# Output projection and first norm interleaved with the first 96 codebook lookup slots of a transformer layer (one core)

## What is computed

```python
q, k, v = proj(wq), proj(wk), proj(wv)            # 32 heads of 32, rotary on q and k
out = softmax(causal(q @ k.T / sqrt(32))) @ v
x = layernorm(x + out @ wo.T)                      # the part that the change moves
Wg, Wu, Wd = codebook[idx_gate], codebook[idx_up], codebook[idx_down]
h = silu(x @ Wg.T) * (x @ Wu.T)                    # inner width 2752
x = layernorm(x + h @ Wd.T)
```

## Time and profile before

| | |
|---|---|
| median of 3 runs | 7037.45 us (7036.92 to 7038.21) |
| the profiled execution: its time / its span | 7038.14 us / 7036.0 us |
| TensorE matmul busy | 6852.8 us, 97% of the span |
| VectorE / ScalarE / GpSimd busy | 4982.9 (71%) / 3672.3 (52%) / 5063.2 (72%) |
| TensorE on the chain that ended last | 63% of the span |

### The profile page before, as it was taken

How to read it: one execution, slowest core, us unless ns; L and a number is a source line. 1 busy time by engine, 2 the same in 40 slices (tenths; PEclk the granted TensorE clock), 3 DMA queues, 4 the chain that set the end, 5 groups by cost and what they waited for, 6 DMA issues and landing times.

```text
span 7036.0 us, 109336 instructions
## 1 busy us (share of the span) xinstructions
PE 6852.8 (97%) x29072; PEld 4331.6 (62%) x29072; DVE 4982.9 (71%) x11788; ACT 3672.3 (52%) x6498; POOL 5063.2 (72%) x5316
## 2 busy tenths in 40 slices
PE   7999999999999999999999999999999999999998
PEld 3444666665466656666666666666666666666664
DVE  3320777775299877788877888778887788877864
ACT  0000777774177755555555555555555555555541
POOL 7777777777777777777777777777777777777760
PEclk9999999999999999999999999999999999999999
DMA  4232111112233323333332333333333233333321
GB/s 127 63 90 49 30 33 32 33 31 58 46 88 90 77 63 72 66 70 72 70 71 64 72 74 72 69 66 71 71 71 70 64 72 72 70 72 67 71 59 48
DMA packets 472442, 462.10 MB, mean 66 GB/s; under 512 B 231120, under 2 KB 347728, under 8 KB 467536
## 3 DMA queue, kind: packets, MB, share of 16 engines
q10 hardware_dynamic: 287072, 396.73, 20.0%
q0 software_dynamic: 169984, 22.10, 7.8%
q1 hardware_dynamic: 14832, 36.84, 1.4%
HBM read 398.07 MB, written 57.15 MB: 65 GB/s over the span
## 4 chain that ended last, share of the span: by engine, by line
PE 63%; DVE 2%; issue 1%; ACT 1%; DMA 0%; DVEq 0%; ACTq 0%
PE ps L414 33%; PE ps L442 17%; PE ps L460 9%; PE ps L425 4%; DVE onehot L964 1%; DVE picked L972 1%; PE ps L431 0%; ACT onehot L738 0%; ACT onehot L742 0%; PE ps L534 0%; DVE small L1015 0%; ACT arena L824 0%; DMA arena<-code_low 0%; DVEq L191 0%; DVE big L956 0%
## 5 line engine op out<-in xcount | busy, mean ns | idle before, releaser
L201 POOL DMA_INDIRECT raw<-in_codebook_dram,idx_sb x5312 | 5063.0, 953 | 1763.9 <-issue 1760.9
L414 PE MATMUL ps<-onehot,table 128*128 128x512 f32 x11776 | 3149.5, 416 | 55.4 <-DVE picked L972 28.7
L964 DVE TENSOR_SCALAR_CACHE_REDUCE onehot<-arena,small 128x512 fp32r<-128x512 f32 x3685 | 2514.1, 743 | 786.7 <-PE ps L414 759.2
L414 PEld LDWEIGHTS ps<-onehot,table 128*128 128x128 f32 x11776 | 2172.1, 188 | 944.3 <-issue 312.6
L738 ACT ACTIVATE onehot<-arena,small 128x512 fp32r<-128x512 f32 x2211 | 1435.4, 713 | 1078.7 <-PE ps L414 974.2
L742 ACT ACTIVATE onehot<-onehot,small 128x512 fp32r<-128x512 f32 x2211 | 1425.2, 708 | 0.0
L442 PE MATMUL ps<-big,arena 128*128 128x512 f32 (+1 forms) x2816 | 1281.2, 592 | 1.3 <-DVE big L956 1.3
L972 DVE SCALAR_TENSOR_TENSOR picked<-arena,small,ps 128x512 fp32r<-128x512 f16 x1472 | 1032.2, 743 | 52.7 <-PE ps L414 37.8
L442 PEld LDWEIGHTS ps<-big,arena 128*128 128x128 f32 (+1 forms) x2816 | 524.2, 187 | 514.0 <-issue 477.5
L877 DVE TENSOR_REDUCE small<-ps 128x1 f32<-128x384 f32 (+7 forms) x512 | 374.2, 752 | 434.7 <-PE ps L304 434.6
L460 PE MATMUL ps<-arena 128*128 128x512 f32 (+1 forms) x1408 | 646.0, 595 | 2.2 <-ACT arena L714 1.1
(11 more groups left out here) (70 smaller groups left out, 3117.4 us busy)
## 6 DMA issues: line engine op xcount, KB each, us to landing
arena<-code_low ACTq DMA_DIRECT2D x738, 256.0 KB
arena<-code_high ACTq DMA_DIRECT2D x738, 128.0 KB
raw<-in_codebook_dram,idx_sb POOLq DMA_INDIRECT x5312
gathered_units<-raw SPq DMA_DIRECT2D x40, 512.0 KB
arena<-gathered_units ACTq DMA_DIRECT2D x20, 1024.0 KB
queries_keys<-arena ACTq DMA_DIRECT2D x16, 1024.0 KB, 4.0
arena<-queries_keys ACTq DMA_DIRECT2D x32, 512.0 KB
big<-in_xT_dram ACTq DMA_DIRECT2D x4, 2048.0 KB, 17.4
```

What stands on the lines that cost most here:

```text
L201: pool.indirect_dma_start(raw[:, s, n, :], None, codebook, bass.IndirectOffsetOnAxis(ap=idx_sb[:, s, n:n + 1], axis=0),).then_inc(gathered ...
L414: last = mm(ps[:, bank + c, :], table[:, k, c, :], onehot[:, k, :], start=(k == 0), stop=(k == KLO - 1))
L964: dve.tensor_scalar(onehot[:, k, :], lo_sb[:, s % 2, :], kp_sb[:, k:k + 1], None, ALU.is_equal, ALU.add, accum_out=hits[:, k:k + 1]).then_ ...
```

## The change

The x1 stage no longer stands ahead of the 96 slots. Each of the 16 blocks of tokens gets six slots (BESIDE = 6, numbered q = 0 to 5). TensorE's 16 products of the block are cut by PARTS into 4, 4, 3, 3, 2 and 0, each cut placed ahead of that slot's look-up. The look-ups all use banks 4, 5 and wait for the pick of the slot before; banks 0, 1 take the projection and banks 2, 3 the transposes. VectorE's sum and statistics stand behind slot 4's work, its normalising behind slot 5's. The block's transposes stand behind the fold of slot q = 1 of the next block and ScalarE's copy at q = 2. ScalarE's square root is at q = 5. ScalarE issues the code loads first and the `sel` and `d_raw` loads behind them, all now right after attention.

```diff
+BESIDE = 3 * SLOTS // SB
+PARTS = (0, 4, 8, 11, 14, 16, 16)
...
-            def project(k):
-                past(pe, sum_ready, k - 1)
-                for h in range(2):
-                    for g in range(NG):
-                        last = mm(ps[:, 4 * (k % 2) + h, :], big1[:, g, k * P:(k + 1) * P], wo_sb[:, g, h * N:(h + 1) * N],
-                                  start=(g == 0), stop=(g == NG - 1))
-                last.then_inc(wo_done, 1)
+            def project(k, n0, n1):
+                if n0 == 0:
+                    past(pe, sum_ready, k)
+                for n in range(n0, n1):
+                    h, g = divmod(n, NG)
+                    last = mm(ps[:, h, :], big1[:, g, k * P:(k + 1) * P], wo_sb[:, g, h * N:(h + 1) * N],
+                              start=(g == 0), stop=(g == NG - 1))
+                if n1 == 2 * NG:
+                    last.then_inc(wo_done, 1)
...
-            for unit in range(3):
-                for s in range(SLOTS):
-                    look_up(unit * SLOTS, s, 4 - 4 * (s % 2), 1)
+            pe.wait_ge(wo_in, 16)
+            pe.wait_ge(o_copied, 2 * ROUNDS * PASSES)
+            for k in range(SB):
+                for q in range(BESIDE):
+                    if PARTS[q] < PARTS[q + 1]:
+                        project(k, PARTS[q], PARTS[q + 1])
+                    unit, s = divmod(k * BESIDE + q, SLOTS)
+                    look_up(unit * SLOTS, s)
+                    if k == 0 and q == 0:
+                        pe.wait_ge(sel_ready, 1)
                     if s:
                         fold(unit * SLOTS, unit, s - 1)
                     elif unit:
                         fold(unit * SLOTS - SLOTS, unit - 1, SLOTS - 1)
+                    if k and q == 1:
+                        turn_x1(k - 1)
+                if k == 0:
+                    pe.wait_ge(d_in, 16)
+                    for h in range(CS):
+                        last = nc.tensor.transpose(ps[0:HALF, 2 + h // 4, (h % 4) * P:(h % 4 + 1) * P],
+                                                   d_raw[:, h, :], id_sb[:, :])
+                    last.then_inc(turn_done, 1)
+            turn_x1(SB - 1)
+            pe.wait_ge(x1T_ready, SB)
```

ScalarE and VectorE:

```diff
+            act.wait_ge(o_copied, 2 * ROUNDS * PASSES)
             act.wait_ge(lo_out, 32)
             for s in range(2):
                 load_codes(0, s)
+            act.dma_start(sel_raw, sel).then_inc(sel_in, 16)
+            act.wait_ge(unit_ready, 1)
+            act.dma_start(d_raw, units[0, :, 0:CS * HALF].rearrange("p (h i) -> p h i", h=CS)).then_inc(d_in, 16)
             near(0, 0)
+            for k in range(SB):
+                for q in range(BESIDE):
+                    unit, s = divmod(k * BESIDE + q, SLOTS)
...
+                    if k == 1 and q == 0:
+                        turned(1, HALF, 2)
+                    if k and q == 2:
+                        copy_x1(k - 1)
+                    if q == BESIDE - 1:
+                        deviation(k)
                     near(unit * SLOTS, s + 1)
+            copy_x1(SB - 1)
...
+            for k in range(SB):
+                for q in range(BESIDE):
+                    unit, s = divmod(k * BESIDE + q, SLOTS)
+                    look_up(unit * SLOTS, s)
+                    if q == BESIDE - 2:
+                        norm_sums(k)
+                    if q == BESIDE - 1:
+                        norm(k)
```

More of the change, by code:

```diff
@@ L375, in _ @@
                 weigh(PASSES - 1, ROUNDS - 1, o, False)
-            def project(k):
-                past(pe, sum_ready, k - 1)
-                for h in range(2):
-                    for g in range(NG):
-                        last = mm(ps[:, 4 * (k % 2) + h, :], big1[:, g, k * P:(k + 1) * P], wo_sb[:, g, h * N:(h + 1) * N],
-                                  start=(g == 0), stop=(g == NG - 1))
-                last.then_inc(wo_done, 1)
+            def project(k, n0, n1):
[7 more added lines that the diff above has]
+                    last.then_inc(wo_done, 1)
             def turn_x1(k):
                 pe.wait_ge(x1_ready, k + 1)
-                past(pe, x1T_ready, k - 1)
+                past(pe, x1T_ready, k)
+                if k == 0:
+                    pe.wait_ge(d_ready, 1)
                 for e in range(KT):
-                    last = nc.tensor.transpose(ps[:, 4 * (k % 2) + 2 + e // 4, (e % 4) * P:(e % 4 + 1) * P],
+                    last = nc.tensor.transpose(ps[:, 2 + e // 4, (e % 4) * P:(e % 4 + 1) * P],
                                                x1_blk[:, k % 2, e * P:(e + 1) * P], id_sb[:, :])
                 last.then_inc(x1T_done, 1)
[L395 to L402, removed]
             def look_up(first, s, bank=4, held=0):
@@ L682, in load_block, with copy_x1 @@
                 act.dma_start(x_blk[:, k % 2, :], x_nat[k * P:(k + 1) * P, :]).then_inc(x_in[k % 2], 16)
[L684 to L693, removed]
+            def copy_x1(k):
+                act.wait_ge(x1T_done, k + 1)
+                act.copy(big1[:, :, k * P:(k + 1) * P],
+                         ps[:, 2:4, :].rearrange("p h (e s) -> p (h e) s", e=4)).then_inc(x1T_ready, 1)
+                if k + 2 < SB:
+                    load_block(k + 2)
             def load_gate_up(u, count):
@@ L779, in _ @@
                 load_codes(0, s)
-            turned(1, HALF, 2)
-            act.wait_ge(sel_ready, 1)
+            act.dma_start(sel_raw, sel).then_inc(sel_in, 16)
+            act.wait_ge(unit_ready, 1)
+            act.dma_start(d_raw, units[0, :, 0:CS * HALF].rearrange("p (h i) -> p h i", h=CS)).then_inc(d_in, 16)
             near(0, 0)
-            for unit in range(3):
-                for s in range(SLOTS):
+            for k in range(SB):
+                for q in range(BESIDE):
+                    unit, s = divmod(k * BESIDE + q, SLOTS)
                     next_codes(unit, unit * SLOTS, s)
@@ L924, in _, with norm_sums @@
                     copy_o(PASSES - 1, u, o)
-            for k in range(SB):
+            def norm_sums(k):
                 dve.wait_ge(wo_done, k + 1)
@@ L929, in _ @@
                 x_v = x_blk[:, k % 2, :].rearrange("p (h d) -> p h d", h=2)
-                dve.tensor_tensor(x_v, ps[:, 4 * (k % 2):4 * (k % 2) + 2, :], x_v, ALU.add).then_inc(sum_ready, 1)
+                dve.tensor_tensor(x_v, ps[:, 0:2, :], x_v, ALU.add).then_inc(sum_ready, 1)
                 dve.wait_ge(sum_ready, k + 1)
-                past(dve, x1T_done, k - 1)
                 for h in range(2):
@@ L937, in _, with norm @@
                 dve.bn_aggr(meanvar, stats.rearrange("p n k -> p (n k)")).then_inc(var_ready, 1)
+            def norm(k):
+                past(dve, x1T_done, k - 1)
                 dve.wait_ge(std_ready, k + 1)
@@ L997, in _ @@
                 one_hot(0, 0, k)
-            for unit in range(3):
-                for s in range(SLOTS):
-                    look_up(unit * SLOTS, s, 4 - 4 * (s % 2))
+            for k in range(SB):
[6 more added lines that the diff above has]
+                        norm(k)
             lookup_step(0, HALF, 3 * SLOTS)
```

## The result

The changed kernel takes 6995.1 us (median of 4 runs, 6993.79 to 6998.43) where the kernel before took 7037.5 (7036.92 to 7038.21) beside it: a ratio of 0.994, 95% interval 0.9923 to 0.9958, 42.4 us less. The forecast was 7000.0, in a range of 6988 to 7018.

What follows compares the result with a forecast made beforehand. TensorE's program with its waits was the bound, ScalarE pacing the 96 slots. Start 1693.5, 16 blocks of 41.1, plus 1.7, 3.3, 2.5 and 8.6 gave 2367.2 against 2407.0; less 1.8, 38 saved: 7000.0, range 6988 to 7018.

Steps and rivals of the forecast that it cites:

- first look-up: Start of the 96 slots: first look-up at 1693.5 us, with loads out at about 1687.5 and 2.5 us of TensorE idle.
- a block (a late one): Six slots from look-up to look-up: 7.56, 7.58, 6.71, 5.9, 5.7 and 7.65 us, in all 41.1.
- block 0 over a plain one: First block: no x1 turn (-0.87), fresh one-hots (+0.4), the d_raw turn with its switch (2.15), in all +1.7 us.
- take-outs of units 0 and 1: ScalarE's four outlet copies, 1.20 us in all, push its near late by some 1.7 and 0.8 us: +2.5.
- drain over a plain end: After the last look-up: step 0 starts 10.9 us later where a block would take 7.65, so +3.3 us.
- step 0's first slot: First slot after the drain: 8.6 us kept from the kernel before, where the clock had dropped to 0.50.
- step 0's second slot (with 1.8 for late codes): Look-up ending the changed stretch: summed to 2367.2 us, plus 1.8 for late codes, so 2369, against 2407.0 before.
- The norm's cover: Block end on VectorE: sum and statistics give 7.65 us behind q5; normalising is hidden, or costs 1.0 a block if uncovered.
- Half of the waits: Lower end of the range: 6988 us if half of the waits vanish, 0.85 us a block.
- The clock did not fall in the blocks: Rivals: clock falls once per block, 27 us back, 7027, chance 0.10; or twice, 54 us back, 7054, chance 0.04.
- The waits vanished: Rival: VectorE's chain is shorter without the loop's adds, a block takes 39.4, 27 us less, 6973, chance 0.05.
- The gathers hold nothing: Rival on the kernel's end: gathers or their loads hold it, nothing of the 38 us shows, 7037, chance 0.01.

Runs made afterwards that it cites:

- one-bank run: The kernel before with all look-ups of its 96 slots on banks 4, 5, nothing else changed: 13729.41 us against 13644.89 for the kernel before.
- bunched run: The changed kernel with all 16 products ahead of a block's first look-up: 13692.5 us against 13644.89 for the kernel before.
- both repeats of the changed kernel: The changed kernel unchanged, run again: 13604.19 us against 13644.51 for the kernel before, and on the other chip 6997.53 against 7035.18.
- run without cover: The changed kernel with products 6, 6, 4, 0, 0, 0 and VectorE's sum, statistics and normalising one slot earlier: 13699.34 us against 13644.51 for the kernel before.

## Why the prediction was right

| step | forecast | measured |
|---|---|---|
| first look-up | 1693.5 | 1693.64 |
| a block (a late one) | 41.1 | 40.94 |
| block 0 over a plain one | +1.7 | +0.1 |
| take-outs of units 0 and 1 | +2.5 | +1.0, late codes in it |
| drain over a plain end | +3.3 | +3.9 |
| step 0's first slot | 8.6 | 8.73 |
| step 0's second slot (with 1.8 for late codes) | 2369.0 | 2363.28 |

*The bound was read rightly.* The pace was not TensorE's (ScalarE's by its timeline), and the change puts the wait on VectorE's pick. The one-bank run shows that chain alone at 5.72 us (5.7 forecast), the bunched run shows it in four slots of six, and the turn set into the wait shows that the gap is free.

*The block was right by its parts*: 7.33, 7.56, 6.69, 6.04, 5.85, 7.47 against 7.56, 7.58, 6.71, 5.9, 5.7, 7.65. The last three are VectorE's, and were put 0.14 and 0.15 too short and 0.18 too long; the first, TensorE's, was put 0.23 too long. Blocks 1, 3 and 11 took 41.19 to 41.26.

*The first look-up* came on time because two errors cancel: the loads went out at 1687.05 and not at 1687.5 us, and the look-up came 6.6 us behind them and not 6.0.

*The norm's cover* was as told for the sum and statistics: with a projection beside them they cost next to nothing (the block is 1.55 us over TensorE's own 39.39, and 1.38 of that is the wait at q = 5), and without that cover the wait grows from 1.38 to 3.14 us. The normalising costs nothing behind q = 5: from 2309.65 to 2310.46 us it runs while VectorE would wait for the look-up of 2309.69 to answer. No run took its cover away.

*Block 0 was charged too much.* Its distances were 7.66, 6.71, 6.68, 6.03, 5.86 and 8.07. The term that was off is the `d_raw` turn, put at 2.15 us. I took its 1.89 us from the earlier trace rows, where it stood behind 4.01 us of idle time at half clock. A window of the kernel before, columns as in rows 2:

```profile
1928.00:1930.00 2.00, 0.71 (x4) 0.63 (x5) 0.33 (x1) 0.00 (x0) 1.39 (x3) 0.50 0.90 224
```

In the changed kernel the turn ran in dense work:

```profile
1730.75 1.03 PE L506 MATMUL ps<-id_sb,arena 128*64 128x128 f32 x8
```

That is 1.03 in the row and 0.87 to the next start. It lengthened its distance by 0.60 only, to 8.07 from the 7.47 that VectorE sets; the other 0.27 fitted beside VectorE's chain. A duration from the edge of a stage is a duration at the clock of the edge. In both repeats of the changed kernel block 0 took 43.0, with a first slot of 9.56 to 9.65: there the clock had fallen behind the first wait of 2.95 to 3.21 us. So there some 2 us over a plain block came out as well, by another way and by luck. Step 0's first slot took 9.7 in the repeats and not 8.73, with the clock down for 10.2 us and not 6.8. The two together are 3 us of the difference between 42.4 here and 40.3 and 37.7 there; the rest is open.

*Take-outs and late codes.* ScalarE has slack now, and the first copies (still 1.20 us, at 1918.59) had waited 5.09 us for TensorE's fold: block 5 took 41.97, block 10 nothing more. Of the 2.5 us 1.0 came, and late codes are in it. The copies push ScalarE's issue of the next code loads back, to 1924.68 us, and VectorE then waits for them, the only such wait of the stretch:

```profile
1928.61 0.75 DVE L976 TENSOR_SCALAR_CACHE_REDUCE onehot<-arena,small 128x512 fp32r<-128x512 f32 x1 [1.76 <-DMA arena<-code_low]
```

In the repeats this wait is 1.33 and 1.34 us, and block 5 takes 41.54 to 41.57. So late codes exist, but as one wait that costs a few tenths beyond the take-out and not 1.8; the sum was nearer without that allowance.

*The drain* was 0.6 longer than forecast: I had the clock fall in step 0 but not in the turn before, which took 1.97.

The terms together: from the first look-up to step 0's first pass 660.9 us, 665.1 forecast. Of the 4.2 less, 2.6 are the blocks, 1.6 block 0 and 1.5 the take-outs; the drain takes 0.6 back and blocks 1, 3 and 11 some 0.9. Two of the forecast's bounds do not follow from its own figures. Half of the waits at 0.85 us a block leads to 6986.4 and not 6988. And 719.4 less 630 is 89 us to win and not 85, or some 82 if the 7.05 us of a step's slot are taken off for step 0's first. Neither touches the forecast.

*The rivals.* The clock did not fall in the blocks: it read 1.00 over 652.6 us with a wait of 1.4 in each, 1.72 and 1.78 in two of them, and in the bunched run it held through four waits of 1.3 to 1.4 a block. The Trainium skill (TensorE: Matmul & The Clock Gate, "A second HAM failure mode: psum-queue depth-cycling") has the clock swing with idle moments between such groups. For waits of up to 1.78 us in the blocks the changed kernel's trace does not agree; for the waits of 3.1 us, in the run without cover, the trace does, in 13 blocks of 16. The waits vanished only when the parts and banks were changed for it. The gathers hold nothing: the changed kernel ended 42.6 us earlier with all of them in it.

## What to carry to other kernels

Where two stages are bound by different engines, read from start-to-start distances how long the busy-looking engine really stands, and what loop sets the pace; then sum each slot as the longer of the matmul work and of the other engine's chain. Fill every slot to at least the length of that chain: one bare slot in six cost 1.5 us a block, and all in one place cost the whole gain. Where ends are modelled, a wait can be there without a bracket: compare the start with the end of what it waits for. Before taking a duration from a row, look at what clock it ran, above all behind a long wait.

## What was not expected of the hardware

The second chip ran the same program in 13604 us. Its page for the changed kernel:

```profile
span 13606.3 us, 109335 instructions
...
POOL 7777777777777777777776000000000000000000
PEclk6555555555555555555555999999999999999999
```

As long as GpSimd gathers, to about 7417 us, the program crawls, and TensorE's clock is at 0.50. A piece of the q, k, v projections:

```profile
3001.11 1.01 PE L284 MATMUL ps<-big 128*128 128x512 f32 x1 [1.79 <-issue]
3001.41 1.10 POOL L203 DMA_INDIRECT raw<-in_codebook_dram,idx_sb  x1 [0.30 <-issue]
3002.81 1.10 POOL L203 DMA_INDIRECT raw<-in_codebook_dram,idx_sb  x1 [0.30 <-issue]
3003.91 1.01 PE L284 MATMUL ps<-big 128*128 128x512 f32 x1 [1.79 <-issue]
```

One matmul starts per 2.80 us, in step with two gathers, and waits for nothing but its issue. Behind the last gather everything runs as on the first chip. The changed stretch lies there, from about 8299 us, and its plain blocks take 40.91 to 40.97 us on both chips; that is why the differences carry over. On the first chip the gathers run beside the stretch, and its blocks are no longer for it. What slows TensorE's issue on the second chip is open, and so is whether the gathers are the cause or only run at the same time.
